# A decoder block on one core: cross-attention's first rows, queries and query weights made in self-attention's block

## The chip, the cores and the metric

The kernel runs on one core of one Trainium2 chip. The metric is the device time of one execution in microseconds (us). The shares and times of single instructions come from one profiled execution of the kernel before.

## The reference

A pre-norm decoder block on x of 2 x 2048 rows of 512 (all float32), with a context of 2 x 154 rows of 1024:

```
x = x + attn(layernorm(x))              # 16 heads of 32; each block of 64 queries sees 32 keys,
                                        # queries and keys taken in the order of a Hilbert curve
x = x + xattn(layernorm(x), context)    # 16 heads of 64, 154 keys and one null key
x = x + ffn(layernorm(x))               # 8 experts, one per row, at most 512 rows each

# xattn
q = x @ Wq;  k, v = split(context @ Wkv)          # Wq 512 x 1024, Wkv 1024 x 2048
out = softmax(q @ [null_k, k].T * scale) @ [null_v, v]
out = layernorm(out @ Wout) * ln_scale + ln_bias  # Wout 1024 x 512
```

## The kernel before

The 4096 rows are 32 tiles of 128 rows, in 8 groups of 4 tiles. A float32 product is made of three products of split operands: each operand is cast to a high part (ACT) and the rest is its low part (DVE), and `product` (L65 to L67) multiplies high by high, low by high and high by low. So every weight matrix has to be loaded, cast on ACT and subtracted on DVE before PE can use it, and so has every turned tile.

The program is four blocks with a barrier of all engines between them; nothing of a block starts before all of the one ahead has ended. Every engine's order of work is written out by hand in each block.

- `setup` (0 to 140 us): keys and values of the context, weights and keys of self-attention, small tables, empty rows for the experts.
- `self_attention` (140 to 477 us). For each group i the first tile's step turns the four tiles of group i + 1 (`turn_x`, `xt_copy` on ACT and DVE), and the four steps make its queries, one block of 128 columns each (`queries(i + 1, c)`, 12 products of 128x512). Beside them the tiles of group i go through scores, sums, values and the projection (`project`), whose result is added to x (`residual`, DVE L795) and stored to a scratch tensor x1 (`store`, SP). Row statistics and norms of group i + 2 are made by DVE (`row_stats` L747, `norm` L756) and POOL (`power`), from rows that POOL gathers (`gather`). In the last group there is no next group: nothing is turned and no queries are made.
- `cross_attention` (477 to about 1262 us). Its steps run from group -2 on. First SP loads x1's first tiles into `tiles`, DVE and POOL norm them, PE turns them (L1669), ACT and DVE split them (`xt_copy`, L1188 and L1343). In group -1 SP loads Wq and Wout in four units of 1 MB through one buffer of two places that lies in `prob`, ACT casts them (`split`, L1159), DVE subtracts (`split`, L1302), and PE makes queries 0 to 5 of group 0. The last step of group -1 (step -1 below) makes queries 6 and 7 beside the first scores. From step 0 on each step n makes scores of tile n + 1 in three bursts (`scores`, L1605), their exponentials (`expo`, ACT L1168), the largest and the scaling (`top`, `scale`, DVE L1321, L1329, L1332), turns the probabilities of tile n (L1593), multiplies by the values, and projects tile n - 1 (`output`).
- `experts`: the routed rows, to the end.

Of the buffers, `big_h`, `big_l` (Wq in cross-attention), `tiles`, `turned_h`, `turned_l`, `wide` (queries) and `rows` are made after self-attention's own buffers are given back, and are shared by cross-attention and the experts.

The places that the change touches: the end and the start of `self_attention` on all engines, its `first`, `middle` and `last` steps, `cross_attention`'s `units`, `split`, `run`, and all counts of its semaphores for turned tiles and queries.

Of the kernel before, what the change touches and what calls it, by code (L numbers as in the profile page):

```python
# [69 lines left out]
def decoder_kernel(nc, x, ctx, wqkv, bqkv, wproj, bproj, mapping, wq2, wkv2, null_kv, wout, ln_scale, ln_bias,  # L70
# [11 lines left out]
    with ExitStack() as keep:  # L82
# [34 lines left out]

        stage_a = ExitStack()
        with stage_a:
# [12 lines left out]
            with ExitStack() as st:  # L132
# [3 lines left out]
                      wq_h, wq_l, wp_h, wp_l, bq_col, k1, v1, idx_all, head_pick, head_spread, seg_tab)  # L136
            release_sems()
            with ExitStack() as st:
                self_attention(nc, sem, lambda *a: sb(*a, stack=st), banks, x_rows, x_tiles, x1_tiles, ident, head_mask,
                               minus_half, bproj_b, wq_h, wq_l, wp_h, wp_l, bq_col, k1, v1, idx_all, head_pick,  # L140
                               head_spread, seg_tab)
        release_sems()

        big_h, big_l = sb("big_h", [P, KD, INNER], F32R), sb("big_l", [P, KD, INNER], F32R)
        tiles = sb("tiles", [P, G, D])
        turned_h, turned_l = sb("turned_h", [P, KD, G * P], F32R), sb("turned_l", [P, KD, G * P], F32R)
        wide = sb("wide", [P, 2, KI, G * P])
        rows = sb("rows", [P, 2, G, ROW])
        with ExitStack() as st:
            cross_attention(nc, sem, lambda *a: sb(*a, stack=st), banks, x1_tiles, out_tiles, slots_dram, slot_tiles,  # L150
                            wq2, wout, w1, w2, ident, upper, ones, minus_half, rev, token_int, token_f, lns_b, lnb_b,
# [7 lines left out]
def setup(nc, sem, sb, bank, x_rows, ctx, wqkv, bqkv, wproj, bproj, mapping, wkv2, null_kv, ln_scale, ln_bias, wr, br,  # L159
          slot_tiles, ident, upper, ones, head_mask, minus_half, rev, token_int, token_f, bproj_b, lns_b, lnb_b, br_b,  # L160
          wr_sb, k2, v2_main, v2_rest, wq_h, wq_l, wp_h, wp_l, bq_col, k1, v1, idx_all, head_pick, head_spread,
          seg_tab):
# [4 lines left out]
    raw = sb("raw", [P, 2, 2048])  # L167
    wc_h = sb("wc_h", [P, 2, 8, CB], F32R)
    wc_l = sb("wc_l", [P, 2, 8, CB], F32R)
    ctx_sb = sb("ctx_sb", [P, 3, CTX])  # L170
    ct_h = sb("ct_h", [P, KC, 3 * P], F32R)
    ct_l = sb("ct_l", [P, KC, 3 * P], F32R)


    xk = ctx_sb[:, 0:2, :].rearrange("p a (b d) -> p (a b) d", d=D)
# [3 lines left out]
    v_tmp = sb("v_tmp", [P, 2, D])  # L179
# [46 lines left out]
    with block as block:  # L226
        @block.sync
        def _(sp):
# [6 lines left out]
            for b in range(B):  # L235
                sp.dma_start(ctx_sb[:, b, :], ctx[b, 0:P, :]).then_inc(ctx_loaded[b], 16)
            load(0)
            sp.wait_ge(ctx_zeroed, 1)
            for b in range(B):
                sp.dma_start(ctx_sb[32 * b:32 * b + REM, 2, :], ctx[b, P:LC, :]).then_inc(ctx_loaded[2], 16)  # L240
# [46 lines left out]
        def _(pool):  # L287
            pool.memset(ctx_sb[:, 2, :], 0.0).then_inc(ctx_zeroed, 1)
# [209 lines left out]
        def _(pe):  # L498
# [8 lines left out]
            for r in range(CR):  # L507
                pe.wait_ge(ctx_loaded[r // 2], 16 if r < 4 else 32)
                turn(r, lambda k, r=r: ctx_sb[:, r // 2, (4 * (r % 2) + k) * P:(4 * (r % 2) + k + 1) * P])
# [51 lines left out]
def self_attention(nc, sem, sb, banks, x_rows, x_tiles, x1_tiles, ident, head_mask, minus_half, bproj_b, wq_h, wq_l,  # L561
                   wp_h, wp_l, bq_col, k1, v1, idx_all, head_pick, head_spread, seg_tab):
# [4 lines left out]
    xg = sb("a_xg", [P, G, D])  # L567
    xt_h = sb("a_xt_h", [P, KD, G * P], F32R)
    xt_l = sb("a_xt_l", [P, KD, G * P], F32R)
    qt = sb("a_qt", [P, 2, KD, G * P])  # L570
    k_seg = sb("a_k_seg", [P, 4, KD, NKEY])
    v_seg = sb("a_v_seg", [P, 4, KD * D1])
    prob = sb("a_prob", [P, 2, D])
# [3 lines left out]
    recip_t = sb("a_recip_t", [P, D])  # L577
    mixed = sb("a_mixed", [P, D])
    at_h = sb("a_at_h", [P, 2, KD, P], F32R)
    at_l = sb("a_at_l", [P, 2, KD, P], F32R)  # L580
    xr = sb("a_xr", [P, G, D])
# [8 lines left out]
             "res_biased").split()  # L590
    s = {n: sem("a_" + n) for n in names}
    gathered = [sem(f"a_gathered{k}") for k in range(G)]
    xr_loaded = [sem(f"a_xr_loaded{t}") for t in range(G)]
# [8 lines left out]
    def tiled(n):  # L602
        return 0 <= n < NT

# [4 lines left out]
    with block as block:  # L609
        @block.sync  # L610
        def _(sp):
# [21 lines left out]
        def _(pool):  # L633
# [31 lines left out]
            def step(i, t, n):  # L665
# [7 lines left out]
                if t and there(i + 2):  # L673
# [18 lines left out]
        def _(act):  # L692
# [4 lines left out]
            def q_copy(i, c):  # L697
                act.wait_ge(s["q_done"], KD * i + c + 1)
                act.activation(qt[:, i % 2, c, :], q_bank[c % 2][:, :], ACT.Identity, bias=bq_col[:, c:c + 1])\
# [14 lines left out]

            def step(i, t, n):
                if t == 0:
                    if there(i + 1):
                        xt_copy(i + 1, 0)
                        xt_copy(i + 1, 1)
                    if tiled(n):  # L720
                        expo(n)
                    if there(i + 1):
# [1331 lines left out]
```

## Time and profile before

| | |
|---|---|
| runs | 1472.57 us median of 3 (1470.28 to 1478.46) |
| profiled execution | 1472.92 us, its span 1471.2 us, mean PE clock 0.961 |
| busy PE, PE weight load | 1332.9 us (91%), 1097.2 us (75%) |
| busy DVE, ACT, POOL | 931.4 us (63%), 655.5 us (45%), 396.8 us (27%) |
| DMA | 122.70 MB, 83 GB/s over the span |

The span is the time from the first to the last instruction, 1.7 us less than the execution. PE is busy for 91% of it, so time can only come from the few stretches in which PE has little to do, or from less work on PE. A matmul's end is modelled and its work is pipelined: twelve products of 0.39 us each start 0.23 us apart. The clock is the share of full speed that PE was granted: 1.00 is 2.4 GHz, 0.50 is 1.2 GHz.

### The profile page before, as it was taken

The numbers are of one execution on the slowest core, as the hardware profiler recorded it, in microseconds if no ns is written. First come the engines' busy times: TensorE is split into PE (matmuls) and PEld (weight loads), VectorE is DVE, ScalarE is ACT, GpSimd is POOL, SyncE is SP. The second block draws the span as 40 slices with busy tenths as digits, with TensorE's granted clock in tenths as the row PEclk, the third lists the DMA queues.
The fourth block names the chain that finished last, engine by engine and source line by source line (L and its number), as shares of the span: only waits on it lengthen the run. The fifth ranks groups of instructions, "written<-read, shape, count | busy, mean of one in ns | idle before, by whom it ended". The sixth has DMA issues, their size and how long they took to land. (4 is left out here: it accounts for less than half of the span.)

```text
span 1471.2 us, 31670 instructions
## 1 busy us (share of the span) xinstructions
PE 1332.9 (91%) x12420; PEld 1097.2 (75%) x12420; DVE 931.4 (63%) x1817; ACT 655.5 (45%) x1796; POOL 396.8 (27%) x475
## 2 busy tenths in 40 slices
PE   6997799999997389999999999999999886799998
PEld 6985577777775267878788887888888765587876
DVE  4535676666654636667767777776766686466663
ACT  3336233333331245555555555555555552446462
POOL 2201444444421101211313222221310213334432
PEclk9999899999999589999999999999999998799999
DMA  7545222222211510110201102020100301546340
GB/s 211 168 154 206 64 81 82 88 88 82 80 57 48 200 29 9 37 44 15 95 15 67 50 35 75 16 94 16 66 16 15 130 15 67 199 135 206 127 135 20
DMA packets 74837, 122.70 MB, mean 83 GB/s; under 512 B 17945, under 2 KB 26137, under 8 KB 74694
## 3 DMA queue, kind: packets, MB, share of 16 engines
q1 hardware_dynamic: 66374, 97.11, 20.2%
q0 software_dynamic: 8320, 23.62, 4.6%
q8 instruction: 98, 1.61, 0.4%
q14 instruction: 45, 0.37, 0.1%
HBM read 82.14 MB, written 42.07 MB: 84 GB/s over the span
## 5 line engine op out<-in xcount | busy, mean ns | idle before, releaser
L1168 ACT ACTIVATE b_prob<-bank,b_neg_top 128x155 f32<-128x155 f32 x512 | 192.8, 405 | 138.3 <-DVE b_neg_top L1321 138.3
L65 PE MATMUL bank<-turned_h,big_h 128*128 128x512 f32 x320 | 132.1, 413 | 18.0 <-DVE turned_l L1343 14.5
L1321 DVE TENSOR_REDUCE b_neg_top<-bank 128x6 f32<-128x930 f32 (+1 forms) x96 | 97.4, 1015 | 48.0 <-PE bank L1605 47.4
L67 PE MATMUL bank<-turned_h,big_l 128*128 128x512 f32 x320 | 126.7, 396 | 0.0
L66 PE MATMUL bank<-turned_l,big_h 128*128 128x512 f32 x320 | 126.3, 395 | 0.0
L1593 PEld LDWEIGHTS bank<-ident,b_prob 128*128 128x128 f32 x640 | 94.5, 192 | 33.4 <-DVE b_pt L1338 15.4
L1593 PE MATMUL bank<-ident,b_prob 128*128 128x128 f32 x640 | 105.0, 288 | 13.8 <-DVE b_pt L1338 11.6
L1605 PE MATMUL bank<-k,wide 64*128 64x155 f32 x1024 | 96.8, 319 | 19.2 <-ACT b_prob L1168 17.8
L65 PE MATMUL bank<-b_wo_h,b_ot_h 128*128 128x512 f32 x256 | 113.5, 444 | 0.5 <-DVE b_ot_l L1350 0.4
L1605 PEld LDWEIGHTS bank<-k,wide 64*128 64x128 f32 x1024 | 74.0, 192 | 45.8 <-ACT b_prob L1168 22.4
L1168 ACT ACTIVATION_READ_ACCUMULATOR b_prob<-bank,b_neg_top 128x1 f32 x512 | 105.9, 207 | 0.0
L1332 DVE TENSOR_TENSOR b_prob<-b_prob,b_recip 128x930 f32<-128x930 f32 (+1 forms) x96 | 102.3, 1066 | 3.3
L67 PE MATMUL bank<-b_wo_h,b_ot_l 128*128 128x512 f32 x256 | 101.6, 397 | 0.0
L66 PE MATMUL bank<-b_wo_l,b_ot_h 128*128 128x512 f32 x256 | 100.5, 392 | 0.0
L1183 ACT ACTIVATE b_pt<-bank 128x512 f32<-128x512 f32 x96 | 57.6, 600 | 90.0 <-PE bank L1593 89.9
L1338 DVE COPY b_pt<-bank 128x512 f32<-128x512 f32 x64 | 44.1, 690 | 69.0 <-PE bank L1593 69.0
L1120 POOL TENSOR_TENSOR b_y_rstd<-b_y_var,minus_half 128x1 f32<-128x1 f32 x32 | 17.8, 555 | 254.3 <-DVE b_y_var L1311 254.1
L65 PEld LDWEIGHTS bank<-turned_h,big_h 128*128 128x128 f32 x320 | 61.5, 192 | 31.2 <-DVE turned_l L1343 14.9
L1176 ACT ACTIVATE wide<-bank 128x512 f32<-128x512 f32 x64 | 38.3, 598 | 90.4 <-PE bank L67 90.4
L1120 POOL TENSOR_TENSOR b_w_rstd<-b_w_var,minus_half 128x1 f32<-128x1 f32 x32 | 29.0, 907 | 175.7 <-DVE b_w_var L1311 175.7
L67 PEld LDWEIGHTS bank<-turned_h,big_l 128*128 128x128 f32 x320 | 60.9, 190 | 13.7
L66 PEld LDWEIGHTS bank<-turned_l,big_h 128*128 128x128 f32 x320 | 61.2, 191 | 11.1
(242 smaller groups left out, 3385.3 us busy)
## 6 DMA issues: line engine op xcount, KB each, us to landing
wide<-in_L_ffn_W_dram SPq DMA_DIRECT2D x16, 1024.0 KB, 5.3
slot_rows<-empty_row SPq DMA_DIRECT2D x1, 8256.0 KB, 24.4
raw<-in_L_xattn_Wkv_dram SPq DMA_DIRECT2D x8, 1024.0 KB, 6.2
a_xr<-in_x_dram SPq DMA_DIRECT2D x32, 256.0 KB, 2.7
x_scratch<-a_xr SPq DMA_DIRECT2D x32, 256.0 KB, 2.0
tiles<-x_scratch SPq DMA_DIRECT2D x32, 256.0 KB, 2.9
rows<-x_scratch SPq DMA_DIRECT2D x32, 256.0 KB, 3.7
out_dram<-rows SPq DMA_DIRECT2D x32, 256.0 KB, 2.0
```

Of the source, the lines that this page charges most:

```text
L65: pe.matmul(out, lh, rh, start=first, stop=False)
L66: pe.matmul(out, lh, rl, start=False, stop=False)
L67: return pe.matmul(out, ll, rh, start=False, stop=last)
L1120: pool.tensor_tensor(rstd[kind][:, k:k + 1], var_eps[kind][:, :], minus_half[:, 0:1], ALU.pow)\
L1168: last = act.activation(prob[:, n % 2, j, h:h + 2 * L2 - 1:2], s_banks[:, h, o:o + L2], ACT.Exp, bias=neg_top[:, n % 2, h, j:j + 1], accum ...
L1176: act.activation(qt[:, i % 2, c, :], src, ACT.Copy).then_inc(s["q_evac"], 1)
L1183: act.activation(pt[:, 4 * u:4 * u + 4, :], pt_bank.rearrange("p (c t) -> p c t", c=4), ACT.Copy)\
L1321: dve.tensor_reduce(neg_top[:, n % 2, :, first:end], s_banks[:, :, 0:(end - first) * L2].rearrange("p h (j k) -> p h j k", k=L2), AX.X, AL ...
L1332: dve.tensor_tensor(p, p, heads.rearrange("p h (j k) -> p j k h", k=1) .to_broadcast([P, end - first, L2, 2]), ALU.mult).then_inc(s["s_sca ...
L1338: dve.tensor_copy(pt[:, 4 * u:4 * u + 4, :], pt_bank.rearrange("p (c t) -> p c t", c=4))\
L1593: last = pe.transpose(pt_bank[:, k * P:(k + 1) * P], src, ident[:, :])
L1605: last = pe.matmul(s_banks[:, h, o:o + L2], qt[rows_h, n // G % 2, j, n % G * P:(n % G + 1) * P], k2[rows_h, n // (G * NB), j, :], start=T ...
```

## The change

Queries 0 to 5 of cross-attention's group 0, the norms of its groups 0 and 1, the turning of group 0 and the split of Wq are made in self-attention's block, where they take the places of a ninth group. So that both blocks can hold them, the shared buffers are made before `setup`, and the buffers of setup and self-attention are laid over them. Wout is loaded in one go at the start of cross-attention and split in its step 0, in place: its raw form lies where its low part comes to lie.

```diff
+        big_h, big_l = shared("big_h", [P, KD, INNER], F32R), shared("big_l", [P, KD, INNER], F32R)
+        tiles = shared("tiles", [P, G, D])
+        turned_h, turned_l = shared("turned_h", [P, KD, G * P], F32R), shared("turned_l", [P, KD, G * P], F32R)
+        wide = shared("wide", [P, 2, KI, G * P])
+        rows = shared("rows", [P, 2, G, ROW])
...
 # self_attention
+    xg, xt_h, xt_l = tiles, turned_h, turned_l
+    qt = wide[:, :, 0:KD, :]
+    w_raw = lay("a_w_raw", [P, KD, INNER], F32, "big_l")
...
+    QUERIES = 6
+    SPLIT_AT = (4, 5, 6, 8, 9, 10, 12, 13)
...
 # SP
+            def load_next(n):
+                for k in range(G):
+                    sp.wait_ge(s["x_turned"], n + G + k + 1)
+                    sp.wait_ge(x1_stored[k], 16 * ((n + 2 * G - NT) // G + 1))
+                    sp.dma_start(xg[:, k, :], x1_tiles[:, n + 2 * G - NT + k, :]).then_inc(next_loaded[k], 16)
+
             for n in range(NT):
+                if n == 1:
+                    for k in range(KD):
+                        sp.dma_start(w_raw[:, k, :], wq2[k * P:(k + 1) * P, :]).then_inc(s["w_loaded"], 16)
+                if n in (NT - 2 * G, NT - G):
+                    load_next(n)
                 if n > 0:
                     store(n - 1)
...
 # ACT, at the end of the steps in SPLIT_AT; DVE subtracts at the same place
+            def split(n):
+                if n == SPLIT_AT[0]:
+                    act.wait_ge(s["w_loaded"], 16 * KD)
+                act.activation(piece(big_h, n), piece(w_raw, n), ACT.Copy).then_inc(s["w_high"], 1)
...
 # DVE
             def last(i, n):
                 m = G * (i + 2) + 2
                 if tiled(n):
                     reciprocals(n)
-                if tiled(m):
-                    row_stats(m)
-                    row_stats(m + 1)
-                    norm(m)
+                row_stats(m)
+                row_stats(m + 1)
+                norm(m)
...
-            first(NG, NT)
+            residual(NT - 1)
...
 # PE
             def queries(i, c):
                 pe.wait_ge(s["x_low"], G * (i + 1))
                 need(pe, s["q_evac"], KD * i + c - 1)
+                if i == NG:
+                    pe.wait_ge(s["w_low"], len(SPLIT_AT))
...
-                if there(i + 1):
-                    queries(i + 1, 3)
+                queries(i + 1, 3)
...
-            first(NG, NT)
+            project(NT - 1)
+            for c in range(KD, QUERIES):
+                queries(NG, c)
...
 # cross_attention
+    wo_raw = nc.alloc_sbuf_tensor_at("b_wo_raw", [P, KI, D], F32, offset=wo_place)
+    DONE = 6
+    NU = 4
...
     def run(step):
-
-        for i in range(-2, NG + 1):
+        step(-1, 3, -1)
+        for i in range(NG + 1):
...
 # SP
-                if i == -1 and t == 0:
-                    load_weights()
+                if n == -1:
+                    for u in range(NU):
+                        sp.dma_start(part(wo_raw, u),
+                                     wout[u * 2 * P:(u + 1) * 2 * P, :].rearrange("(k p) n -> p k n", p=P))\
+                            .then_inc(s["raw_loaded"], 16)
...
 # ACT, between expo(n + 1, 1) and expo(n + 1, 2)
+                if n == 0:
+                    split(0)
+                    split(1)
                 if not late(i, t) and tiled(n - 1):
                     w_copy(n - 1)
                 if t == 3 and querying:
                     q_copy(i + 1, 7)
+                if n == 0:
+                    split(2)
+                    split(3)
...
 # DVE
                 if tiled(n):
                     pt_copy(n, 4)
+                if n == 0:
+                    split(0)
+                    split(1)
...
                 if tiled(n + 1):
                     scale(n + 1, 1)
                     top(n + 1, 2)
+                if n == 0:
+                    split(2)
+                    split(3)
```

**PE where self-attention ends and cross-attention begins.** `wp` and `a_at` are the projection of self-attention, `wr_sb` the router's weights, `turned` and `big` the turned tiles and Wq, `k` and `wide` the keys and queries of cross-attention. The branches stand at the barrier. Before:

```order
L67 MATMUL bank<-wp_h,a_at_l 128x512
L609 UNCONDITIONAL_BRANCH
L1577 UNCONDITIONAL_BRANCH
L1791 MATMUL bank<-wr_sb,ones 128x8 x4
L1669 MATMUL bank<-ident,tiles 128x128 x16
L65 MATMUL bank<-turned_h,big_h 128x512
L66 MATMUL bank<-turned_l,big_h 128x512
L67 MATMUL bank<-turned_h,big_l 128x512
```

And now:

```order
L67 MATMUL bank<-turned_h,big_l 128x512
L634 UNCONDITIONAL_BRANCH
L1617 UNCONDITIONAL_BRANCH
L1830 MATMUL bank<-wr_sb,ones 128x8 x4
L1645 MATMUL bank<-k,wide 128x155 x6
L65 MATMUL bank<-turned_h,big_h 128x512
L66 MATMUL bank<-turned_l,big_h 128x512
L67 MATMUL bank<-turned_h,big_l 128x512
```

Sixteen transposes and six blocks of queries (72 products) no longer stand between the barrier and the first scores; two blocks of queries stand ahead of the barrier, behind the last projection, and the other four among the steps of the last group.

**SP where self-attention begins.** `a_xr` are the rows of x for the residual, `slot_rows` the experts' empty rows. Before:

```order
L280 DMA slot_rows<-empty_row 128x32x516
L226 UNCONDITIONAL_BRANCH
L610 UNCONDITIONAL_BRANCH
L615 DMA a_xr<-in_x_dram 128x512 x4
L619 DMA x_scratch<-a_xr 128x512
L615 DMA a_xr<-in_x_dram 128x512
```

And now:

```order
L296 DMA slot_rows<-empty_row 128x32x516
L242 UNCONDITIONAL_BRANCH
L635 UNCONDITIONAL_BRANCH
L640 DMA a_xr<-in_x_dram 128x512 x4
L657 DMA a_w_raw<-in_L_xattn_Wq_dram 128x1024 x4
L644 DMA x_scratch<-a_xr 128x512
L640 DMA a_xr<-in_x_dram 128x512
```

The four loads of Wq stand ahead of the first store, and nothing on SP is waited for before them.

**DVE in step 0 of cross-attention.** `b_neg_top` is the result of `top`, `b_recip` and `b_prob` that of `scale`, `b_pt` a copy of turned probabilities. Before:

```order
L1321 TENSOR_REDUCE b_neg_top<-bank 128x2x3
L1338 COPY b_pt<-bank 128x512
L1306 BN_STATS b_x_stats<-tiles 128x6
L1309 BN_AGGR b_x_mv<-b_x_stats 128x2
L1311 TENSOR_SCALAR b_x_var<-b_x_mv 128x1
L1329 RECIPROCAL b_recip<-b_total 128x2x3
L1332 TENSOR_TENSOR b_prob<-b_prob,b_recip 128x3x310
L1321 TENSOR_REDUCE b_neg_top<-bank 128x2x2
L1555 TENSOR_SCALAR tiles<-tiles,b_x_mv,b_x_rstd 128x512
L1329 RECIPROCAL b_recip<-b_total 128x2x2
L1332 TENSOR_TENSOR b_prob<-b_prob,b_recip 128x2x310
```

And now:

```order
L1362 TENSOR_REDUCE b_neg_top<-bank 128x2x3
L1379 COPY b_pt<-bank 128x512
L1343 TENSOR_TENSOR b_wo_l<-b_wo_raw,b_wo_h 128x1024 x2
L1347 BN_STATS b_x_stats<-tiles 128x6
L1350 BN_AGGR b_x_mv<-b_x_stats 128x2
L1352 TENSOR_SCALAR b_x_var<-b_x_mv 128x1
L1370 RECIPROCAL b_recip<-b_total 128x2x3
L1373 TENSOR_TENSOR b_prob<-b_prob,b_recip 128x3x310
L1362 TENSOR_REDUCE b_neg_top<-bank 128x2x2
L1343 TENSOR_TENSOR b_wo_l<-b_wo_raw,b_wo_h 128x1024 x2
L1595 TENSOR_SCALAR tiles<-tiles,b_x_mv,b_x_rstd 128x512
L1370 RECIPROCAL b_recip<-b_total 128x2x2
```

Two subtractions of 128x1024 stand ahead of the row statistics and of `scale(1, 1)`, and two more behind `top(1, 2)`, ahead of `scale(1, 2)`. On ACT all four casts stand together behind the exponentials of the second burst.

## Rows read from the trace of the kernel before

**Rows 1.** Page, part 2: the span in 40 slices of 36.8 us.
```profile
PE   6997799999997389999999999999999886799998
...
PEclk9999899999999589999999999999999998799999
```

**Rows 2.** Windows: us; busy PE, PEld, DVE, ACT, POOL; PE clock, DMA share, GB/s.
```profile
398.70:436.80 38.10, 37.72 (x694) 29.16 (x692) 20.81 (x33) 12.25 (x20) 10.80 (x20) 1.00 0.18 58
437.60:469.70 32.10, 26.42 (x562) 20.42 (x560) 17.31 (x27) 7.32 (x12) 8.12 (x12) 0.89 0.15 52
461.90:468.50 6.60, 6.58 (x80) 5.39 (x81) 1.39 (x2) 1.23 (x2) 0.00 (x0) 0.50 0.01 2
477.50:506.70 29.20, 5.20 (x24) 3.97 (x24) 17.79 (x28) 9.80 (x8) 2.19 (x4) 0.52 0.72 252
506.70:509.50 2.80, 2.73 (x7) 2.15 (x7) 1.93 (x6) 0.00 (x0) 0.55 (x1) 0.50 0.00 0
```

**Rows 3.** Order of time on PE, start of cross-attention (start, length in us).
```profile
477.57 1.03 PE L1791 MATMUL bank<-wr_sb,ones 128*128 128x8 f32 x8 [3.97 <-PEq L95]
...
506.77 0.79 PE L65 MATMUL bank<-turned_h,big_h 128*128 128x512 f32 x1 [14.45 <-DVE turned_l L1343]
...
524.63 1.07 PE L1605 MATMUL bank<-k,wide 64*128 64x155 f32 x12
```

**Rows 4.** Order of time on PE: two steps after a pause.
```profile
461.92 2.07 PE L904 MATMUL bank<-a_recip,head_spread 128*128 128x128 f32 x8 [2.94 <-DVE a_recip L779]
...
538.10 1.92 PE L1605 MATMUL bank<-k,wide 64*128 64x155 f32 x12 [2.58 <-ACT b_prob L1168]
```

**Rows 5.** Order of time on DVE and ACT, where self-attention begins and ends.
```profile
148.95 0.69 DVE L747 BATCH_NORM_STATS2 a_stats<-a_xg 128x6 f32<-128x512 f32 x1 [0.35 <-DMA a_xg<-in_x_dram,idx_all]
...
473.64 0.69 DVE L795 TENSOR_TENSOR a_xr<-bank,a_xr 128x512 f32<-128x512 f32 x1 [3.24 <-PE bank L67]
...
511.14 0.60 ACT L1176 ACTIVATE wide<-bank 128x512 f32<-128x512 f32 x1 [7.10 <-PE bank L67]
...
513.86 0.60 ACT L1176 ACTIVATE wide<-bank 128x512 f32<-128x512 f32 x1 [2.12 <-PE bank L67]
```

**Rows 6.** Waits between 180 and 480 us (total, times, longest).
```profile
DVE a_total L777 <- PE bank L897: 39.8, 28, 2.1
```

**Rows 7.** Order of time on ACT and DVE: the splits of weights.
```profile
486.68 1.90 ACT L1159 ACTIVATE big_h<-b_prob 128x2048 fp32r<-128x2048 f32 x1
...
490.80 4.48 DVE L1302 TENSOR_TENSOR big_l<-b_prob,big_h 128x2048 fp32r<-128x2048 f32 x2
```

**Rows 8.** DMA issues of the whole span (KB each, us to landing).
```profile
x_scratch<-a_xr SPq DMA_DIRECT2D x32, 256.0 KB, 2.0
tiles<-x_scratch SPq DMA_DIRECT2D x32, 256.0 KB, 2.9
...
a_xg<-in_x_dram,idx_all POOLq DMA_INDIRECT x32, 3.8
```

**Rows 9.** Tile ctx_sb between 40 and 140 us, its gathers in setup.
```profile
DMA to landing us min/median/max: 4.1/4.9/7.9
```

**Rows 10.** Order of time on DVE, ACT, PE in step 0.
```profile
551.97 0.68 DVE L1338 COPY b_pt<-bank 128x512 f32<-128x512 f32 x1
...
553.92 0.42 ACT L1168 ACTIVATE b_prob<-bank,b_neg_top 128x155 f32<-128x155 f32 x1
...
554.45 0.19 DVE L1329 RECIPROCAL b_recip<-b_total 128x6 f32<-128x6 f32 x1 [0.73 <-ACT b_prob L1168]
...
554.68 1.96 DVE L1332 TENSOR_TENSOR b_prob<-b_prob,b_recip 128x930 f32<-128x930 f32 x1
...
557.39 0.41 ACT L1168 ACTIVATE b_prob<-bank,b_neg_top 128x155 f32<-128x155 f32 x1 [2.44 <-DVE b_neg_top L1321]
...
559.03 1.07 PE L1605 MATMUL bank<-k,wide 64*128 64x155 f32 x12 [0.97 <-ACT b_prob L1168]
...
560.09 0.66 PE L1593 MATMUL bank<-ident,b_prob 128*128 128x128 f32 x4
```

More of the change, by code:

```diff
@@ L116, in decoder_kernel, with shared, lay @@
         v2_rest = sb("v2_rest", [P, B, 4, 2 * D2])
+        place = {}
+        def shared(name, shape, dt=F32):
+            place[name] = nc.sbuf_base
+            return sb(name, shape, dt)
+        def lay(name, shape, dt, over, skip=0):
+            return nc.alloc_sbuf_tensor_at(name, shape, dt, offset=place[over] + skip)
+        big_h, big_l = shared("big_h", [P, KD, INNER], F32R), shared("big_l", [P, KD, INNER], F32R)
[3 more added lines that the diff above has]
+        rows = shared("rows", [P, 2, G, ROW])
         stage_a = ExitStack()
@@ L589, in self_attention @@
              "sum_eps sum_recip recip_spread recip_evac a_norm a_high a_low proj_done x1_made "
-             "res_biased").split()
+             "res_biased w_loaded w_high w_low").split()
     s = {n: sem("a_" + n) for n in names}
     gathered = [sem(f"a_gathered{k}") for k in range(G)]
+    next_loaded = [sem(f"a_next_loaded{k}") for k in range(G)]
     xr_loaded = [sem(f"a_xr_loaded{t}") for t in range(G)]
@@ L672, in step @@
                         gather(G * (i + 2) + k)
-                if t and there(i + 2):
+                if t and i < NG:
                     for k in ((0,), (1,), (2, 3))[t - 1]:
@@ L736, in step @@
                     at_copy(n)
+                if n in SPLIT_AT:
+                    split(n)
             for i in range(-1, NG):
@@ L813, in first @@
                     at_rest(n)
+                if n in SPLIT_AT:
+                    split(n)
             def middle(i, t, n):
@@ L871, in queries @@
                 need(pe, s["q_evac"], KD * i + c - 1)
+                if i == NG:
+                    pe.wait_ge(s["w_low"], len(SPLIT_AT))
                 for k in range(KD):
-                    last = product(pe, q_bank[c % 2][:, :], [a[:, k, c * P:(c + 1) * P] for a in (wq_h, wq_l)],
+                    last = product(pe, q_bank[c % 2][:, :],
+                                   [a[:, k, c * P:(c + 1) * P] for a in ((big_h, big_l) if i == NG else (wq_h, wq_l))],
                                    [a[:, k, :] for a in (xt_h, xt_l)], k == 0, k == KD - 1)
@@ L947, in first @@
                     values(n, n + 2)
-                if there(i + 1):
-                    queries(i + 1, 0)
+                queries(i + 1, 0)
             def middle(i, t, n):
@@ L957, in middle @@
                     values(n, n + 2)
-                if there(i + 1):
-                    queries(i + 1, t)
+                queries(i + 1, t)
             def last(i, n):
@@ L977, in _, with cross_attention @@
                 last(i, G * i + 3)
-            first(NG, NT)
-def cross_attention(nc, sem, sb, banks, x1_tiles, out_tiles, slots_dram, slot_tiles, wq2, wout, w1, w2, ident, upper,
+            project(NT - 1)
+            for c in range(KD, QUERIES):
+                queries(NG, c)
+def cross_attention(nc, sem, sb, banks, x1_tiles, out_tiles, slots_dram, slot_tiles, wout, w1, w2, ident, upper,
                     ones, minus_half, rev, token_int, token_f, lns_b, lnb_b, br_b, wr_sb, k2, v2_main, v2_rest, wq_h,
```

215 lines of the change are left out of this document (94 added, 121 removed).

## The prediction

> **What bounds the kernel now.** I read the 40 slices first. Three of them break a PE row of 9s: the slice around 140 us, and the slices from 478 to 552 us, where the granted clock falls too [rows 1]. The first lies between setup and self-attention, the others between self-attention and cross-attention. Then the windows [rows 2]. A steady group of self-attention (four tiles of 128 rows) takes 38.1 us and keeps PE busy for 37.72 of them, so PE is the bound there. The last group has no next group to turn and no queries to make: 32.1 us for 26.42 us of work, a fifth of it idle, at a clock of 0.89. From 477.5 to 506.7 PE works 5.2 us of 29.2, while DMA moves 252 GB/s, and DVE and ACT normalise four tiles and split 4 MB of weights, one after the other. Last I read the order of time on PE [rows 3]: cross-attention's first instruction starts at 477.57, its first query product only at 506.77, its first scores at 524.63. So 47.06 us pass in which PE does 16 transposes and six of the eight blocks of queries of the first group, and nothing else can run. From the scores on, PE and the softmax take turns until 540.0, where the scores at 538.10 end (step -1, 15.4 us) [rows 4]; then comes step 0, and from 560.09 PE is hardly idle again in this stage [rows 10].
>
> I make the sum against the profiled execution, 1472.92 us (span 1471.2); the median of the runs shown is 1472.57, 0.35 lower. A measurement of this kernel can tell about 0.5% (7.4 us) from no change.
>
> **1. The start of cross-attention: -46.0 us.** Loads, norms and turns of tiles 0 to 3, the split of Wq and queries 0 to 5 are gone from this block. PE's order there is now the two sums of the router's weights (L1791, 1.0 us in [rows 3]), then scores at once: they wait only for the queries of the block before. 47.06 - 1.1 = 46.0. The 2 MB of Wout load beside step -1 and are first needed in step 0, over 15 us later; at the 252 GB/s of [rows 2] they take 8 us, so no wait.
>
> **2. Self-attention's last group becomes a full one: +5.2 us.** It now turns the four tiles and makes queries 0 to 3, which is what every steady group does, so I price it by the steady group: 38.1 us, less 0.85 for the scores of a next tile that isn't there, against the 32.1 us that stand there now. That is 13 us of added PE work for 5.2 us, because it fills waits, and because the clock should not fall in it: before, after 2.94 us idle, L904 took 2.07 us and the clock was 0.50 for 6.6 us [rows 2, 4].
>
> **3. Queries 4 and 5 behind the last projection: +3.5 us.** A block of queries is 12 products; two evacuations of such blocks lie 2.72 us apart [rows 5], and up to 2.8 in self-attention. Two of them are 5.6 us, with the evacuation 6.4. They cover what stood there alone: the last residual (from 473.64, 0.69 us), its store (2.0 us to land) and the barrier, after which PE starts at 477.57 [rows 3, 5, 8]. The tail behind the last product was 3.9 us and becomes 6.4 plus 1.2 of barrier (3.2 from the residual's end to 477.57, less the 2.0 of the store): 7.6, so +3.7; taken as 3.5, since the shorter copy overlaps the barrier a little.
>
> **4. The eight small splits of Wq: 0.** On ACT and DVE they stand last in a tile's work. DVE waits for the sums of the next tile in all 28 tiles seen, 1.4 us each time [rows 6]; a split of 128x512 takes DVE 0.69 at most (a 128x2048 one is 2.24, [rows 7]). ACT idles longer. If that cover were gone each would cost its own 0.7 us, 5.5 in all. Norms and powers of tiles 0 to 7 are those of a steady group. The stores and loads that SP now holds behind its waits for turned tiles (eight loads of x1) are needed a tile later.
>
> **5. The load of Wq at the head of self-attention: +1.5 us (0 to 4.1).** SP waits for nothing before these 2 MB: they go out right behind four loads of x, while POOL issues the first four gathers, for which DVE waits (0.35 us for the second even now [rows 5]), and with DVE the whole block. No row has this load there. The nearest below is the present start, gathers landing in 3.8 us [rows 8]; the nearest above are setup's gathers of the same size beside weight loads, 4.1 to 7.9 us, 4.9 median [rows 9]. 4.9 - 3.8 would be 1.1 and 7.9 - 3.8 is 4.1; four gathers compete, so I take 1.5.
> The Trainium skill (DMA: Bandwidth & Descriptors, Queues, rings and completion order) says that each DMA engine takes turns between the queues that it has work for. By that the gathers share with the 2 MB and the sum stays as below; served in order of issue, the later ones would stand behind up to 8 us of load at the 252 GB/s of [rows 2], and the sum would be some 5 us more. No row of this place decides it yet.
>
> **6. The start of step -1 on a cold PE: +1 us (0 to 2.5).** The barrier leaves PE idle some 2 us. After the idle stretch before 506.77 the clock was 0.50 until 509.5 [rows 2], and 2.7 us at half clock cost 1.4. Here a part of it falls in waits for the softmax.
>
> **7. The splits of Wout inside step 0: +4.8 us (3 to 6).** This is the term that the change adds. Before, they ran inside the 47 us; now four of 128x1024 stand in ACT's order behind the exponentials of the second burst of tile 1, and in DVE's two ahead of `scale(1, 1)` and two ahead of `scale(1, 2)`. From [rows 7] a 128x1024 split is about 0.95 us on ACT and 1.15 on DVE. DVE is done with its copy at 552.65 [rows 10]; ACT is done with the burst at 554.4 and with the first split at 555.4. DVE's two then end at 557.7, and its row statistics at 558.9, where `scale(1, 1)` began at 554.45. Scale and top(1, 2) follow to 561.0, ACT's last burst ends at 562.7 instead of 558.9, DVE's other two splits at 563.3, a norm 563.8, `scale(1, 2)` at 564.8 instead of 560.0. PE's transposes of tile 1 wait for exactly that: 560.09 becomes about 564.9. PE has nothing in its order to put there, and behind it PE is the bound, so it is paid in full. Below, 3: the scale that took 1.96 us takes 1.1, and the 0.73 of wait ahead of it is gone. Above, 6: each split is as long as its share of the 2.24 and waits once more for ACT.
>
> **8. The clock after that pause: +2 us (0 to 3.3).** PE will sit idle about 4.6 us between its values and scores(2, 0) (it was 0.97 before the row at 559.03) and one more before the transposes. Rows show a clock of 0.50 for 2.8 to 6.6 us after pauses of 2.94 us and more [rows 2, 4]; such a stretch loses half its length, 1.4 to 3.3.
> The Trainium skill speaks against the change here (TensorE: Matmul & The Clock Gate, HAM oscillation — how this bites in real kernels): a pause in a dense stream of matmuls sends the clock back to 1.2 GHz, and work has to earn it back. By it the loss is certain, not likely, and the sum is 1446.2 with the term at 3.3; without it, as after the pause of 0.97 us, the term is 0 and the sum 1442.9. The trace agrees with the page as far as it goes: at 538.10, after 2.58 us of pause, twelve score products took 1.92 us, where those at 559.03 took 1.07 [rows 4, 10].
>
> **Sum:** -46.0 + 5.2 + 3.5 + 0 + 1.5 + 1 + 4.8 + 2 = -28.0. 1472.92 - 28.0 = **1444.9 us**. With 7.7 to 10.0 for terms 2 and 3 together and the ends given, all lower ends make -35.3, 1437.6 us, and all upper ones -20.1, 1452.8 us.
>
> **Rivals.**
> A. *More is given back than I count* (0.17): the small splits of term 4 delay a step now and then, term 5 is 4.1 us, term 8 is 3.3, and group 0 of cross-attention starts with DVE behind. For it: in self-attention DVE works 20.8 of 38.1 us and ACT and POOL lie between each of its steps [rows 2]. Upper ends of terms 2, 3 and 6 to 8, the 4.1 of term 5 and half of term 4's 5.5 give 1455 us.
> B. *Less is given back* (0.07): DVE and ACT catch up inside step 0, the clock stays; terms 5 to 8 come to 3 instead of 9.3: 1438.6 us.
> C. *A wait takes the place of the one removed* (0.04): the rows of x1 come through SP, behind stores that wait for projections. DVE takes row statistics in a fixed order, and if a load is late there the softmax of that tile stops. Eight tiles at 3 us are 24: 1469 us, no change. Against it: the load goes out once its buffer is turned, its statistics are asked for about a tile later (38.1 / 4 = 9.5 us), and such loads land in 2.9 us [rows 8].
> D. *Slower* (0.03): one mechanism, the places. All big buffers of setup and self-attention (weights, turned tiles, queries) lie at other addresses of SBUF; if a product of 128x512 or an ACT or DVE pass over them ran at a lower rate, each of the first 478 us would pay. 6% is 28.7 us and eats the gain, 7.5% is 36 and gives 1480: slower from there. At 10% it is 1493 us. Against it: cross-attention reads these shared buffers already, at 2.72 us for twelve products [rows 5].
> That the change doesn't do what it says is little to be feared: the order on PE shows scores as the second thing in the block.
>
> **Numbers.** 0.69 for the forecast, A 0.17, B 0.07, C 0.04, D 0.03. The range from 1436 to 1456 holds the forecast's own ends, B and most of A. Faster by over 0.5% (below 1465) are forecast, A and B: 0.93. Within 0.5%: C, 0.04. Slower: D, 0.03.
>
> **What would show each step right or wrong.** From cross-attention's first PE instruction to its first scores about 1 us, and no query product before them (1). The last group 37 to 38 us, PE at 0.98 (2). From the last projection's end to cross-attention's first instruction 7.5 us (3). DVE still waiting for PE before most sums, none of its waits ending with a_w_raw (4). The first row statistics of self-attention 1 to 4 us later behind setup's end (5). A pause of 4 to 5 us on PE in step 0, ended by DVE or ACT, and half clock behind it (7, 8). If that pause is missing, or if products take 0.25 us instead of 0.23, the sum is wrong.

## The result, and the profile after

The changed kernel takes **1449.61 us** (median of 4 runs, 1449.34 to 1450.39), against 1473.16 for the kernel before in the same measurement (4 runs, 1470.28 to 1478.46): ratio 0.9837, 95% interval 0.9808 to 0.9865. That is 23.5 us less; 28.0 were forecast (1444.9 us), and the time lies within the range, about halfway between the forecast and rival A's 1455. The profiled execution took 1450.39 us, its span is 1448.7 against 1471.2. In the two later measurements, with other kernels beside it, the change gave 27.2 us (1488.77 to 1461.61) and 28.2 us (1474.6 to 1446.43).

The slices of the page of the changed kernel, each 36.2 us:

```profile
PE   6998499999999879999999999999999985899998
PEclk9999699999999979999999999999999997799999
DMA  7446412222222200101102011020100302545430
```

Of the three holes between self-attention and cross-attention [rows 1] one shallow one is left, an 8 and a 7 where 7, 3 and 8 stood. Around 140 us two slices of 7 have become an 8 and a 4. Slices say where to look, not how much. For that I cut both executions at the same events (first gather of self-attention on POOL, first turn on PE, start of the last group's first score burst, start of the last residual on DVE, cross-attention's first instruction on PE, its first scores, the start of the last `scale` of each step) and compare the pieces. "Again" is the changed kernel in the last measurement below.

| piece, us | before | after | difference | term: forecast | again |
|---|---|---|---|---|---|
| setup, to the first gather | 142.17 | 145.78 | +3.6 | none | 140.34 |
| first gather to first turn | 10.40 | 14.32 | +3.9 | 5: +1.5 | 14.12 |
| steady self-attention | 284.21 | 284.09 | -0.1 | 4: 0 | 284.31 |
| last group, to the last residual | 36.86 | 41.53 | +4.7 | 2: +5.2 | 41.59 |
| residual to cross-attention's first PE instruction | 3.93 | 7.13 | +3.2 | 3: +3.5 | 7.13 |
| from there to the first scores | 47.06 | 0.96 | -46.1 | 1: -46.0 | 0.96 |
| step -1 | 13.66 | 14.48 | +0.8 | 6: +1 | 14.24 |
| step 0 | 20.94 | 26.15 | +5.2 | 7: +4.8 | 25.53 |
| step 1 | 20.59 | 21.72 | +1.1 | 8: +2 | 22.41 |
| step 2 and the rest | 891.38 | 892.54 | +1.2 | none | 889.67 |

The eight terms together measure -27.3 where -28.0 was forecast, and the whole span -22.5. The difference is +3.6 in setup, which the change does not touch but for the places of its buffers, and +1.2 from step 2 on.

**The start of cross-attention.** Order of time on PE of the changed kernel, for [rows 3]:

```profile
492.85 1.03 PE L1830 MATMUL bank<-wr_sb,ones 128*128 128x8 f32 x8 [1.68 <-PEq L95]
493.81 1.92 PE L1645 MATMUL bank<-k,wide 64*128 64x155 f32 x12
```

Scores come 0.96 us behind the block's first instruction, and no query product between. They take 1.92 us instead of the 1.07 of the first scores before the change, at half the clock: it was 0.51 from 493.80 to 495.75.

**The last two groups of self-attention.** Windows of the changed kernel (columns as in [rows 2]): a steady group, the last group, and the products behind the pause of step 0.

```profile
404.00:442.00 38.00, 37.62 (x691) 29.46 (x690) 26.69 (x49) 12.26 (x20) 13.72 (x25) 1.00 0.27 86
444.20:485.70 41.50, 40.24 (x702) 31.67 (x702) 27.02 (x49) 11.91 (x20) 10.08 (x16) 1.00 0.22 72
532.40:538.00 5.60, 4.62 (x21) 3.85 (x22) 5.05 (x8) 2.01 (x6) 0.00 (x0) 0.50 0.00 0
```

The last group, up to its last residual, keeps PE busy for 40.24 of 41.5 us at a clock of 1.00; it had 0.89 in the shorter window of [rows 2].

**The first gathers.** Order of time on DVE: the row statistics of tiles 0 to 3 of self-attention.

```profile
152.37 0.69 DVE L796 BATCH_NORM_STATS2 a_stats<-tiles 128x6 f32<-128x512 f32 x1 [8.90 <-DMA tiles<-in_x_dram,idx_all]
...
155.28 0.69 DVE L796 BATCH_NORM_STATS2 a_stats<-tiles 128x6 f32<-128x512 f32 x1 [1.81 <-DMA tiles<-in_x_dram,idx_all]
...
157.06 0.69 DVE L796 BATCH_NORM_STATS2 a_stats<-tiles 128x6 f32<-128x512 f32 x1 [0.68 <-DMA tiles<-in_x_dram,idx_all]
...
158.49 0.69 DVE L796 BATCH_NORM_STATS2 a_stats<-tiles 128x6 f32<-128x512 f32 x1 [0.33 <-DMA tiles<-in_x_dram,idx_all]
```

The transfers of the changed kernel between 138 and 162 us (40 slices of 0.6 us; then each issue, KB, median us to landing):

```profile
DMA  0000000000000059998779999999989997410000
GB/s 0 0 0 0 0 0 0 0 0 0 0 0 0 7 229 403 352 270 205 195 273 358 362 352 369 382 403 376 376 348 389 416 416 294 164 68 0 0 0 0
...
a_w_raw<-in_L_xattn_Wq_dram SPq DMA_DIRECT2D x4, 512.0 KB, 10.0
a_xr<-in_x_dram SPq DMA_DIRECT2D x4, 256.0 KB, 4.0
tiles<-in_x_dram,idx_all POOLq DMA_INDIRECT x4, 8.4
```

All four gathers are waited for, where only the first and, for 0.35 us, the second were [rows 5]. They land in 6.6 to 8.8 us, 8.4 in the median, where the first four of the kernel before took 4.2 to 5.4; three of them are slower than even the slowest gather of setup [rows 9]. The DMA engines are busy for 7 tenths and more of the time for 12 us.

**Step 0.** Order of time on ACT and DVE of the changed kernel, for [rows 10]:

```profile
524.20 3.92 ACT L1202 ACTIVATE b_wo_h<-b_wo_raw 128x1024 fp32r<-128x1024 f32 x4
...
525.31 2.36 DVE L1343 TENSOR_TENSOR b_wo_l<-b_wo_raw,b_wo_h 128x1024 fp32r<-128x1024 f32 x2 [2.76 <-ACT b_wo_h L1202]
...
528.67 0.18 DVE L1370 RECIPROCAL b_recip<-b_total 128x6 f32<-128x6 f32 x1
528.88 1.13 DVE L1373 TENSOR_TENSOR b_prob<-b_prob,b_recip 128x930 f32<-128x930 f32 x1
529.93 0.80 DVE L1362 TENSOR_REDUCE b_neg_top<-bank 128x4 f32<-128x620 f32 x1
530.64 3.23 DVE L1343 TENSOR_TENSOR b_wo_l<-b_wo_raw,b_wo_h 128x1024 fp32r<-128x1024 f32 x2
533.79 0.53 DVE L1595 TENSOR_SCALAR tiles<-tiles,b_x_mv,b_x_rstd 128x512 f32<-128x512 f32 x1
```

And on PE: the scores of tile 2, and the turns of tile 1's probabilities behind them.

```profile
532.41 1.92 PE L1645 MATMUL bank<-k,wide 64*128 64x155 f32 x12 [4.44 <-ACT b_prob L1210]
535.30 1.12 PE L1633 MATMUL bank<-ident,b_prob 128*128 128x128 f32 x4 [0.98 <-DVE b_prob L1373]
```

DVE waits 2.76 us for ACT's first split, then works without a stop, and PE stands idle for 4.44 us and 0.98 more. The four splits take ACT 3.92 us, the two pairs DVE 2.36 and 3.23, where 2.3 was priced for each.

### The profile page after: what moved, and what is told of

It is laid out like the page before. It is cut to its first block and busy times, and to the rows that moved or that the text cites. A ratio compares the mean times of both kernels' runs of the same rounds, so it can differ in the third digit from the quotient of the medians.

```text
span 1448.7 us, 31686 instructions
## 1 busy us (share of the span) xinstructions
PE 1334.8 (92%) x12420; PEld 1100.6 (76%) x12420; DVE 932.1 (64%) x1825; ACT 656.6 (45%) x1804; POOL 400.2 (28%) x475
## 5 line engine op out<-in xcount | busy, mean ns | idle before, releaser
L1218 ACT ACTIVATE wide<-bank 128x512 f32<-128x512 f32 x58 | 34.7, 598 | 72.7 <-PE bank L67 72.6
```

The source lines that it names most:

```text
L1218: act.activation(qt[:, i % 2, c, :], src, ACT.Copy).then_inc(s["q_evac"], 1)
```

## The experiments

Two theories were held against each other first. **L**: the change does what its terms say, and the missing part is the load of Wq's 2 MB in the gathers' way (term 5), with chance in setup. **P**: the new places of the buffers cost time throughout setup and self-attention (rival D). Segments are cut as in the table above.

**The changed kernel once more**, beside the next three.

> The changed kernel itself, as the reference for the others. Its profile showed setup 3.6 us longer than before and self-attention's first transposes 3.9 us later behind the first gather. Theory L (the load of Wq stands in the gathers' way, setup's 3.6 us are chance of its first weight loads): about 1449.6 us; setup's length moves by 2 us or more between the two profiles of this kernel, the 3.9 us stay within 0.5. Theory P (the places of the buffers cost both): both stay, 3.6 and 3.9.

1461.61 us (1457.03 to 1465.42, 6 runs), before 1488.77 (1481.64 to 1499.16, 17 runs): ratio 0.982 (0.9785 to 0.9854). Gain and loss stand where they stood: 14.14 us from gather to first turn, 41.55 for the last group and 7.13 for the joint (from the last residual to cross-attention's first PE instruction), 26.31 and 22.97 for steps 0 and 1. Setup took 140.04 us instead of 145.78 with the same program: its +3.6 is no cost of the change. New is steady self-attention at 299.18 us instead of 284.09. Every kernel of this measurement shows that, so the levels of the two are not comparable, only kernels within one.

**The load of Wq later.**

```diff
             for n in range(NT):
-                if n == 1:
+                if n == 2:
                     for k in range(KD):
                         sp.dma_start(w_raw[:, k, :], wq2[k * P:(k + 1) * P, :]).then_inc(s["w_loaded"], 16)
```

> The 2 MB load of Wq goes out behind the first store of self-attention (n == 2) and no longer at its head. Theory L: from the first gather to the first transposes 10.4 us as before the change, not 14.3, so 3.9 us less than the change: 1445.7 us; no wait for the load at the first split (tile 4 is 25 us later). Theory P: the start stays at 14.3 us, 1449.6 us. If the rows of x or the gathers of a later group stand behind the load instead, up to 3 us come back in self-attention's first groups.

Measured 9.82 us from gather to first turn, below the 10.40 of before. Order of time on DVE, the first two row statistics of self-attention:

```profile
148.52 0.69 DVE L796 BATCH_NORM_STATS2 a_stats<-tiles 128x6 f32<-128x512 f32 x1 [7.50 <-DMA tiles<-in_x_dram,idx_all]
...
149.55 0.69 DVE L796 BATCH_NORM_STATS2 a_stats<-tiles 128x6 f32<-128x512 f32 x1
```

Only the first gather is waited for now. The whole 3.9 us of this piece (4.3 against the change beside it) were the load; none of it is the turn's or the norm's. Nor does it come back later: steady self-attention took 298.99 us, and 299.18 in the change beside it. The time, 1459.25 us (1452.0 to 1464.08, 6 runs; ratio 0.9799, 0.976 to 0.9838), is 2.4 below the change's, with overlapping runs: the place is shown, its worth in the whole is not resolved by this run alone.

**The splits of Wout ahead of step 0**, at the end of step -1, behind the last exponentials on ACT and the last scale on DVE.

```diff
-                if n == 0:
-                    split(0)
-                    split(1)
...
-                if n == 0:
-                    split(2)
-                    split(3)
...
+                if n == -1:
+                    for u in range(NU):
+                        split(u)
```

> The four splits of Wout stand at the end of step -1, behind the last exponentials of tile 0 on ACT and the last scaling on DVE, instead of in step 0. There ACT idles 3.1 and DVE 3.5 us, the four take 3.7 and 4.6. If the splits in step 0 cost 5.2 us and the half clock behind the pause 1.1: step 0 takes 20.8 us again instead of 25.4 (less 1 us that the splits now stick out of the pause), no pause of 4.4 us on PE before the scores of tile 2, in all 4.5 to 5.5 us less than the change: 1444 to 1445. Rival (PE's first steps are bound elsewhere, the pause only moves): within 1.5 us of the change.

Step 0 fell to 22.27 us, step 1 to 20.61, step -1 is 14.29. Order of time on PE, the same scores:

```profile
543.00 1.06 PE L1639 MATMUL bank<-k,wide 64*128 64x155 f32 x12 [0.98 <-ACT b_prob L1210]
```

The pause is 0.98 us, as it was 0.97 before the change, and the scores take 1.06 us: with this pause the slow clock behind it goes too, and step 1 is as short as before the change. But the slow clock is not gone from step 0. Windows (columns as in [rows 2]) from the first scores to the end of step 1, of this run and of the change, and the beginning of this run's step 0:

```profile
506.63:563.80 57.17, 48.71 (x336) 39.42 (x336) 35.80 (x54) 32.92 (x119) 5.24 (x5) 0.85 0.22 77
```

```profile
493.81:556.16 62.35, 50.36 (x336) 41.06 (x336) 35.72 (x54) 32.83 (x119) 6.20 (x5) 0.84 0.20 71
```

```profile
521.40:535.00 13.60, 10.38 (x51) 8.39 (x50) 10.54 (x14) 9.36 (x23) 0.00 (x0) 0.50 0.25 73
```

The clock is 0.50 for 13.6 us there, behind a pause of 2.53 us before the scores of tile 1 and through pauses of 1.03 and 2.19 in the turns, and the mean over the three steps is 0.85 against the change's 0.84. This step is still 1.3 us longer than before the change (20.94), where the splits did not stand at all. Why the slow stretch lasts so long here was not tried.
Terms 7 and 8 together are thus worth 5.0 us against the profile of the change (26.15 + 21.72 - 22.27 - 20.61), 6.4 against its second one. 1454.01 us (1453.3 to 1459.73, 5 runs; ratio 0.9765, 0.9728 to 0.9803), 7.6 below the change in the medians, with overlapping runs and intervals.

**The new places alone**: the kernel before, with setup's and self-attention's buffers laid over the shared ones as in the change, and nothing moved.

```diff
-    raw = sb("raw", [P, 2, 2048])
-    wc_h = sb("wc_h", [P, 2, 8, CB], F32R)
+    raw = lay("raw", [P, 2, 2048], F32, "rows")
+    wc_h = lay("wc_h", [P, 2, 8, CB], F32R, "wide")
...
-    v_tmp = sb("v_tmp", [P, 2, D])
+    v_tmp = lay("v_tmp", [P, 2, D], F32, "big_l", 12288)
```

> The kernel before with the new places of its buffers and nothing else: setup's and self-attention's buffers laid over the shared ones, all work where it was. Theory L: as the kernel before, 1472.6 within 3 us, first transposes 10.4 us behind the first gather. Theory P: 3.6 us more in setup and 3.9 at the start of self-attention, 1480 us. Were matmuls slower from the new places, each steady group of self-attention would take more than 38.1 us.

1489.26 us against 1488.77 (12 and 17 runs), ratio 0.9999 (0.9969 to 1.0029). Theory P (7.5 us, 0.5%) is excluded by the interval, and rival D with it: places cost nothing that could be measured. This run also shows what term 2 was measured against. The window behind the pause of its last group (columns as in [rows 2]), and then the first row behind that pause in the order of time on PE:

```profile
479.00:485.60 6.60, 5.73 (x88) 4.49 (x89) 2.08 (x3) 1.23 (x2) 0.00 (x0) 1.00 0.03 8
```

```profile
478.98 1.16 PE L918 MATMUL bank<-a_recip,head_spread 128*128 128x128 f32 x8 [2.94 <-DVE a_recip L793]
```

The pause is the same 2.94 us as in [rows 4], but here the clock stayed at 1.00, and the last group took 34.00 us instead of 36.86. So 2.9 us of the 36.86 go with a fall of the clock that came in one execution and not in another of the same work (one profile of each; the two kernels differ only in the places of their buffers). Against the execution without it, term 2 would be +7.5, not +4.7.

**All three costs taken out at once**: late load, early splits, and the fifth block of queries ahead of the last projection.

```diff
                 if tiled(n):
                     spread_recip(n)
                     values(n, n + 1)
                     project(n - 1)
+                if n == NT - 1:
+                    queries(NG, KD)
...
             project(NT - 1)
-            for c in range(KD, QUERIES):
+            for c in range(KD + 1, QUERIES):
                 queries(NG, c)
```

> The change with three edits: the load of Wq's 2 MB one tile later in self-attention (as in the run e1), the four splits of Wout at the end of step -1 of cross-attention (as in e2), and the fifth block of queries ahead of the last projection instead of behind it. Theory S (the three costs stand apart and add up): setup's end to first transposes -3.9 to -4.4 us against the change; steps -1, 0 and 1 together -5.5 (as e2 against the profile of the change: 14.29 + 22.27 + 20.61 against 14.48 + 26.15 + 21.72); last group and joint together -0.9, since the pause of 0.88 us ahead of the last projection is filled; in all -10 us, 0.7% below the change in the same job. Theory T (they share one reserve: what is saved ahead is given back by the rest of cross-attention): the segments show the savings, the rest behind step 2 grows by as much (e1 and e2 both had a rest longer by 0.4 to 1.7 us than the change's 871.24), and the time falls by 3 to 5 us only.

**1436.61 us** (1435.88 to 1437.71, 5 runs); before 1474.6 (1471.05 to 1476.37, 9 runs): ratio 0.9747 (0.9734 to 0.976). The change itself, in the same measurement, has 0.9815 (0.98 to 0.983). The intervals lie apart: this version beats both kernels, the change by 9.8 us in the medians. Against the change's profile of the same measurement the pieces give -3.5 (10.64 instead of 14.12), -1.2 (last group and joint 47.54 instead of 48.72), +0.5 (0.96 to 1.42, the first eight small products at half clock) and -3.9 instead of -5.5 (steps -1 to 1, 58.32 instead of 62.18; step -1 alone is 1.1 longer): 8.1 of the 10 expected. The two profiled executions differ by 5.4 us only, that of the change being the fastest of its four runs (1442.05); the runs of the two do not overlap. Theory S holds: T expected 3 to 5 us in the time, and 9.8 came. The rest from step 2 on is 1.2 us longer than in the change's profile and 1.7 shorter than in the first one. With the late load and the early splits alone it was 3.4 and 4.8 us longer than in the change's profile beside them, but two profiles of the change itself differ by 3.1 there, so a small giving back is neither shown nor excluded.

**All eight blocks of queries in self-attention** (`QUERIES = 8`, `DONE = 8`, and step -1 makes none).

> The change with all eight blocks of the first group's queries in self-attention instead of six; step -1 of cross-attention then makes none. Theory A (each block costs its 2.72 us of PE wherever it stands, and what stands behind the last projection covers nothing any more beyond the first block): last group and joint +5.5 us, step -1 shorter by 0.7 to 1.5 only, since PE waits there for the softmax of tile 0 anyway; in all +4 to +4.8 us against the change. Rival B (PE is the bound in step -1 too, so the blocks are moved at no price): step -1 -5.4 us, in all 0.

Last group and joint took 54.11 us, +5.4 against the change beside it, as both theories have it; step -1 took 14.38 us instead of 14.24. Nothing came back, not even the 0.7 of theory A. Rows of PE in step -1:

```profile
498.13 1.92 PE L1645 MATMUL bank<-k,wide 64*128 64x155 f32 x12 [3.66 <-ACT b_prob L1210]
...
503.65 1.41 PE L1645 MATMUL bank<-k,wide 64*128 64x155 f32 x8 [3.60 <-ACT b_prob L1210]
```

Two pauses of 3.66 and 3.60 us stand where blocks 6 and 7 stood. Windows over the same 16.2 us of the step (from 0.6 us ahead of the first scores), of this run and of the change beside it:

```profile
492.80:509.00 16.20, 6.41 (x49) 5.39 (x50) 6.85 (x10) 6.26 (x32) 1.26 (x1) 0.59 0.54 194
```

```profile
487.85:504.05 16.20, 12.45 (x75) 9.47 (x75) 6.85 (x10) 7.35 (x34) 1.29 (x1) 0.86 0.57 194
```

The granted clock is 0.59 there, where the change's is 0.86. The two blocks lie there at no price; moved, they cost 2.7 us each in these pieces. 1449.04 us (1447.89 to 1450.99, 4 runs; ratio 0.9835, 0.9818 to 0.9851) is 2.6 more than the change, less than the 4 to 4.8 expected, with overlapping intervals: the direction is as expected, the size in the whole is not resolved.

**The fifth block of queries ahead of the last projection, alone.**

> The change with one edit: the fifth block of queries is made ahead of the last projection instead of behind it. Theory A (the pause of 0.88 us on PE ahead of the last projection is filled by it and nothing else moves): last group to last residual +1.8 (2.7 of products less 0.9), joint -2.7 to -2.9, sum of the two -0.9 to -1.1 us. Rival B (the tail is then bound by the last residual, its store and the barrier, 3.9 us as before the change, and by one block of queries): the joint can't fall below 4 to 4.5, so the sum is 0 to -0.3.

Last group 43.15 us (+1.56), joint 4.38 (-2.75): together -1.2, against -0.9 to -1.1 expected by theory A. Rival B's floor for the joint is there, 4.38 us, but it does not undo the gain. In the whole it can't be seen: 1444.72 us (1442.12 to 1445.8) against 1446.43 (1442.05 to 1447.57), 4 runs each.

**The change, beside these three.**

> The change itself, as the kernel to compare the other three with on the same chip. Segments as in its two profiles so far: steady self-attention 284.1 or 299.2 (if the longer one is a matter of the chip or the hour, all four kernels of this job show the same one; if it is chance by execution, they differ among themselves); last group and joint 48.7; step 0 26.2; step 1 21.7 to 23.0.

1446.43 us, ratio 0.9815. Steady self-attention took 284.31 us here, and 284.30 to 285.12 in the other three, against 298.99 to 300.29 in all four of the first measurement. The longer one comes with the measurement (another chip and another hour, which these runs can't tell apart), not by chance of one execution.

## Why the prediction was right, and where it was off

**Term 1** (-46.0) measured -46.1. It is the whole gain, and the easiest to price: a stretch in which PE had 5.2 us of work in 29, read from two start times.

**Terms 2 and 3** (+5.2 and +3.5) measured +4.7 and +3.2. Pricing the last group by a steady one, and the queries by the distance of two evacuations, held within 0.5 us. (The prediction's 37 to 38 us for the last group are of a shorter window than the piece of the table; 36.86 + 5.2 = 42.1 is the figure to set against 41.53.) But the fall of the clock that made the old group 2.9 us longer was taken for a property of the kernel; the run with the places alone shows the same work and the same pause without it. The forecast was made from the very profile that it is compared with; against an execution without the fall, its 5.2 would have missed by 2.3. The 7.7 to 10.0 that the prediction allows for the two terms together is worked out nowhere in it; they measured 7.9.

**Term 4** (0) measured -0.1 over 284 us. The eight small splits cost nothing, though each took DVE 0.78 us and not "0.69 at most", and none waited for the load: DVE still waits for the sums of nearly every tile, as in [rows 6]. The waits of the changed kernel from 180 to 480 us (total, times, longest):

```profile
DVE a_total L826 <- PE bank L950: 37.5, 31, 1.6
```

**Term 5** (+1.5) was mis-sized: it measured +3.9, 3.7 to 3.9 in the profiles of the change, close to the upper end of 4.1. The step that failed is "four gathers compete, so I take 1.5". It went by a median from setup, where the DMA engines were busy for 4 to 7 tenths of a slice, not full, and took off 3.8 us, the median of all 32 gathers, where the four at this place took 4.2 to 5.4 even before. A count of bytes would have done better: 1 MB of x, 2 MB of Wq and 1 MB of gathers stand before the fourth row statistics, and the slices from 151.2 to 158.4 us show 348 to 416 GB/s, gathers and load together. Four MB at that rate are 10 to 12 us (an estimate), and the fourth gather's statistics begin 12.7 us behind the first gather. The place is shown by the late load, which gives all of it back.
By the Trainium skill (DMA: Bandwidth & Descriptors, Queues, rings and completion order) gathers and load take turns. The trace agrees: the fourth gather, issued at 149.62, is there at 158.49, while the last of the four loads, issued before it at 148.46, took 11.6 us and landed at 160.1: the gather did not wait behind the whole load. What was wrong is how little I took sharing to cost: 2 MB alone would take 5 to 6 us at that rate (an estimate), and 3.7 to 3.9 of them were paid.

**Term 6** (+1) measured +0.8 and +0.6; in the profile of the change between these two step -1 was no longer than before the change (13.61).

**Terms 7 and 8** (+4.8 and +2) measured +5.2 and +1.1 in the first profile, +4.6 and +1.8 in the last, +5.4 and +2.4 in the one between: 6.3, 6.4 and 7.8 together, 6.8 forecast. The chain was as forecast: ACT's splits, DVE's wait for the first, `scale` and `top` behind them, a pause of 4.44 us on PE (4.6 forecast), then half the clock. The early splits remove this pause and the slow clock behind it, but they bring a slow stretch of 13.6 us at the head of step 0, so the mean clock of steps -1 to 1 stays where the change had put it (0.85 and 0.84; it was 0.91 before the change).
On the clock the Trainium skill (TensorE: Matmul & The Clock Gate, HAM oscillation — how this bites in real kernels) was right to speak against the change here: in each profile with the pause of 4.4 us the clock fell within it or less than 1 us behind it, and step 1 is 1.1 to 2.4 us longer; ahead of the same scores, a pause of 0.98 us left it at 1.00. The 3.3 us that the prediction worked out for that case were above what was measured. And for a pause of 2.94 us the traces show both, 0.50 once and 1.00 once.

**The rivals.** A counted on many small costs; of its parts only term 5 came near its upper end, and the small splits cost nothing. Its 1455 us was not reached. B needed DVE and ACT to catch up inside step 0; they did not. C, waits for the rows of x1, would show in the steady group, 38.0 us (38.1 before), and in step 2, which takes 21.30 us in both kernels: neither grew. D is excluded by its own run.

**The sum against the time.** The terms give -27.3; the first measurement's profile adds +3.6 in setup and +1.2 from step 2 on. ACT's waits for the weights of setup (`raw`) were 13.4 us in it, 11.0 in the profile before and 9.5 in the last one. That accounts for 2.4 of setup's 3.6 us, but why those loads landed later stays open. So the time came out within 5 us of the forecast with one term 2.4 us too small and 4.8 us from pieces that no term covers; in the two later measurements, where setup was not long, the gain was the 28.0 forecast within 1 us. That the eight terms miss by 0.7 us only is partly luck: term 5 is 2.4 and term 7 0.4 above the forecast, the other six together 2.1 below it. (One reading of the page was short: the prediction counts three slices that break PE's row of 9s, but [rows 1] has more of them, a 7 at 441 us among them; no term rests on it.)

## What to carry to other kernels

Work that fills a stage's empty head is worth moving to where the engine waits anyway, but each piece by itself: blocks 0 to 5 of the queries paid together, and blocks 6 and 7, which already stood in a wait, would have cost 2.7 us each in their pieces for nothing. What is pushed aside has to land somewhere as well: the two things this change only displaced, the Wq load and the Wout splits, cost 3.5 to 4.3 and 3.9 to 6.4 us that another place gives back. And a pause that is removed can take its slow clock along and still leave one elsewhere: look at the clock of the whole stage, not only behind the pause. A load put in front of transfers that the stage waits for is priced by all the bytes in flight at the rate that the full engines reached (348 to 416 GB/s here), not by the latency of such a transfer elsewhere.

## What the hardware showed that I had not expected

In the first measurement of experiments steady self-attention was 15 us longer in every kernel, the one with only its buffers moved among them. PE's waits from 182 to 462 us, of the changed kernel there:

```profile
PE bank L940 <- issue: 6.7, 18, 0.4
```

and its order of time in one burst of 64 small score products:

```profile
186.34 0.84 PE L940 MATMUL bank<-wide,a_k_seg 32*32 32x64 f32 x43
...
187.59 0.32 PE L940 MATMUL bank<-wide,a_k_seg 32*32 32x64 f32 x6 [0.41 <-issue]
188.32 0.32 PE L940 MATMUL bank<-wide,a_k_seg 32*32 32x64 f32 x6 [0.41 <-issue]
189.05 0.35 PE L940 MATMUL bank<-wide,a_k_seg 32*32 32x64 f32 x9 [0.41 <-issue]
```

Such a burst takes 0.8 us to the next row as a rule. There, 7 of the block's 32 took 2.0 to 3.4 us, and the 7 add some 13 of the 15 us. In the profiles of the first and the last measurement none did. In these bursts PE stops for 0.4 us every six to nine products, and waits for nothing that the profile shows. At the end of two of them or just behind the clock fell as well, in all four kernels. Windows (columns as in [rows 2]) of the changed kernel:

```profile
269.60:273.10 3.50, 3.39 (x16) 2.64 (x17) 2.32 (x5) 0.63 (x1) 0.29 (x1) 0.51 0.36 119
351.50:355.00 3.50, 3.50 (x10) 2.72 (x9) 2.22 (x5) 0.63 (x1) 1.02 (x2) 0.51 0.27 80
```

It touches both sides of a comparison alike, so ratios within a measurement hold, but times of two measurements of this kernel can't be set against each other. Its cause was not tried.
